# Single-precision zeros for the products that clear the counting banks of a four-layer graph network

## The reference, cut to what matters

```python
edge_index = jnp.stack([src, dst])
x = _layernorm(x + _L0_gnn_ref(x, edge_index, edge_attr_128, ...), axis=-1)
x = _layernorm(x + _L1_gnn_ref(x, edge_index, ...), axis=-1)      # two _gat_conv
x = _layernorm(x + _L2_gnn_ref(x, src, dst, ...), axis=-1)        # agg = segment_sum(h[src], dst)
x = _layernorm(x + _L3_gnn_ref(x, edge_attr_128, ..., src, dst), axis=-1)
```

## Time and profile before

| | us |
|---|---|
| median of three executions (lowest to highest) | 3548.91 (3539.84 to 3549.04) |
| the profiled execution | 3545.56 |
| its span | 3543.7 |
| TensorE busy (share of the span) | 2663.5 (75%) |
| VectorE busy | 2171.4 (61%) |
| ScalarE busy | 1652.8 (47%) |
| GpSimd busy | 1575.3 (44%) |

### The profile page before, as it was taken

How to read it: one execution, slowest core, us unless ns; L and a number is a source line. 1 busy time by engine, 2 the same in 40 slices (tenths; PEclk the granted TensorE clock), 3 DMA queues, 4 the chain that set the end, 5 groups by cost and what they waited for, 6 DMA issues and landing times.

```text
span 3543.7 us, 48598 instructions
## 1 busy us (share of the span) xinstructions
PE 2663.5 (75%) x11507; PEld 1959.5 (55%) x11507; DVE 2171.4 (61%) x5184; ACT 1652.8 (47%) x3627; POOL 1575.3 (44%) x1656
## 2 busy tenths in 40 slices
PE   6777778757777777567777764999998995677766
PEld 4665665434444444334444454777777884566654
DVE  5888886655555555645555567443455546666668
ACT  2887886434444444344444453442222344444443
POOL 4777770277765530177776530000000003777770
PEclk9999999855555555555555555999999997888886
DMA  6555550144443331244444321776677774555550
GB/s 205 155 160 156 161 159 27 38 107 103 99 98 95 89 75 37 58 105 101 99 100 96 89 67 56 246 270 206 225 265 260 270 281 158 154 159 154 159 153 25
DMA packets 391112, 489.16 MB, mean 138 GB/s; under 512 B 168377, under 2 KB 265710, under 8 KB 385888
## 3 DMA queue, kind: packets, MB, share of 16 engines
q1 hardware_dynamic: 324934, 288.34, 26.7%
q0 software_dynamic: 63088, 192.63, 19.9%
q10 hardware_dynamic: 2828, 5.18, 0.5%
HBM read 384.00 MB, written 101.90 MB: 137 GB/s over the span
## 4 chain that ended last, share of the span: by engine, by line
PE 43%; DVE 20%; POOL 12%; issue 10%; DMA 8%; ACT 3%; DVEq 2%; SPq 1%; ACTq 0%; POOLq 0%
PE ps L979 11%; POOL y_and_h L725 10%; DMA rows<-in_ea_swept 7%; PE ps L1060 7%; PE ps L995 6%; PE ps L857 6%; PE ps L991 4%; DVE y_and_h L1690 3%; DVE big L1662 3%; PE ps L943 2%; DVE ps L1682 2%; POOL big L711 2%; ACT w_sb L1419 2%; DVE ps L2169 1%; PE ps L793 1%
## 5 line engine op out<-in xcount | busy, mean ns | idle before, releaser
L711 POOL DMA_INDIRECT big<-table_gat,src_idx x832 | 809.3, 973 | 749.0 <-DMA table_gat<-y_and_h 343.2
L1662 DVE TENSOR_TENSOR big<-big,ps 128x257 f32 (+3 forms) x1664 | 592.6, 356 | 236.3 <-PE ps L979 17.4
L1419 ACT ACTIVATE w_sb<-ps 128x200 uint16 x784 | 262.1, 334 | 757.9 <-PE ps L995 756.7
L725 POOL DMA_INDIRECT y_and_h<-table_pool,src_block x391 | 374.8, 958 | 177.1 <-issue 118.9
L696 POOL DMA_INDIRECT big<-table_mlp,src_block x391 | 371.3, 950 | 158.1 <-issue 116.8
L1466 ACT ACTIVATE big<-big 128x3432 f32<-128x3432 uint16 (+1 forms) x72 | 210.1, 2919 | 476.7 <-PE ps L1060 476.7
L2023 DVE TENSOR_TENSOR big<-w_sb,extra 128x512 bf16<-128x512 bf16 (+1 forms) x392 | 179.1, 498 | 340.7 <-PE ps L995 340.5
L740 POOL DMA_DIRECT2D big<-adj x36 | 19.2, 533 | 802.1 <-ACT big L1466 703.8
L995 PE MATMUL ps<-big 128*128 128x200 bf16 x784 | 277.6, 354 | 77.8 <-ACT w_sb L1419 74.5
L857 PE MATMUL ps<-w_sb,ea_sb 128*128 128x256 f32 x832 | 210.2, 396 | 127.2 <-DVE y_and_h L1690 116.7
L1060 PE MATMUL ps<-big,y_and_h 128*128 128x264 f32 (+1 forms) x1200 | 289.4, 389 | 0.0
(11 more groups left out here) (344 smaller groups left out, 5162.8 us busy)
## 6 DMA issues: line engine op xcount, KB each, us to landing
big<-adj POOLq DMA_DIRECT2D x33, 1650.0 KB, 8.1
rows<-in_ea_swept SPq DMA_DIRECT2D x194, 256.0 KB, 3.4
adj<-w_sb SPq DMA_DIRECT2D x784, 50.0 KB
ea_sb<-in_ea_blocks SPq DMA_DIRECT2D x416, 64.0 KB
ea_sb<-rel_rows SPq DMA_DIRECT2D x208, 128.0 KB
prefix_blocks<-rows SPq DMA_DIRECT2D x97, 256.0 KB, 2.2
rows<-prefix_blocks SPq DMA_DIRECT2D x97, 256.0 KB, 3.5
below_blocks<-ea_sb SPq DMA_DIRECT2D x97, 256.0 KB, 2.7
```

The lines of the kernel that those rows point to most:

```text
L711: pool.indirect_dma_start(ring[:, step % GAT_RING, :], None, table[k], bass.IndirectOffsetOnAxis(src_idx[:, step:step + 1], 0))\
L725: pool.indirect_dma_start(pool_rows[q][:, i, :], None, table["pool"], bass.IndirectOffsetOnAxis(src_block[:, block:block + 1], 0)).then_in ...
L1419: act.activation(staging[:, (4 * quad + j) % STAGED, :], ps[:, 6:8, :][:, bass.ds(halves_of[j + 1], 1), 0:CW].rearrange("p o n -> p (o n)" ...
L1662: dve.tensor_tensor(to, to, bank_of(j), ALU.add).then_inc(accumulated, 1)
```

## The change

The clearing product of each counting step reads its two rows of zeros as single-precision words instead of as bfloat16 ones. Shapes (1 x 128 by 1 x 200), banks, waits and order stay, and so does the value, zero.

```diff
--- before.py
+++ after.py
@@ -309,7 +309,6 @@
         step_chunk, step_key = chain[:, 56:60], chain[:, 60:64]
         staging = w_sb[:, 0:STAGED * CW // 2].bitcast(U16).rearrange("p (s n) -> p s n", s=STAGED)
         count4 = w_sb[:, 1600:1600 + 2 * CW].bitcast(BF16).rearrange("p (n q) -> p n q", q=4)
-        zeros_b = zeros[:, :].bitcast(BF16)
         quads_at = GAT_RING_AT + GAT_RING * ROW["gat1"] + 256 * MARKS
         lo4 = [part_of_big(quads_at + b * 656, 256).bitcast(BF16).rearrange("p (n q) -> p n q", q=4) for b in range(2)]
         col4 = [part_of_big(quads_at + b * 656 + 256, 400).bitcast(BF16).rearrange("p (n q) -> p n q", q=4) for b in range(2)]
@@ -989,7 +988,7 @@
                     if j == 0:
                         pe.wait_ge(quad_ready, quad + 1)
                     pe.matmul(ps[:, 6:8, :][:, ::-1, :][:, bass.ds(halves_of[j], 1), 0:CW].rearrange("p o n -> p (o n)"),
-                              zeros_b[0:1, 0:P], zeros_b[0:1, 0:CW], start=True, stop=True, skip_group_check=True)
+                              zeros[0:1, 0:P], zeros[0:1, 0:CW], start=True, stop=True, skip_group_check=True)
                     if step:
                         pe.wait_ge(step_read, step)
                     pe.matmul(ps[:, 6:8, :][:, bass.ds(halves_of[j + 1], 1), 0:CW].rearrange("p o n -> p (o n)"),
```

## The result

The changed kernel takes 3884.68 us (median of 4 runs, 3881.96 to 3886.64) against 3544.38 us of the kernel before (4 runs, 3535.55 to 3549.04): a ratio of 1.096, 95% interval 1.094 to 1.099. It is slower by 340 us. The profiled executions, 3545.56 and 3881.96 us, differ by 336. The forecast was 3944 us with 3800 to 4020: the side and the range hold, and the sum is 59 us too large (395 against 336).

The account below looks back on a forecast made before the run. TensorE at 1.2 GHz was taken to bound both attention passes. 533 us of longer clearing products, less 86 (ScalarE), 37 (VectorE) and 15 (GpSimd) hidden, gave +395 us: forecast 3944 us, range 3800 to 4020.

Parts of the forecast that it names:

- What bounds the kernel: Both attention passes: TensorE at 1.2 GHz, 73% busy, its lines holding 63% and 56% of the chain of waits.
- Step 1: The bfloat16 clearing product in the passes today: 0.28 us from its weight load to the next product's.
- Step 2: Single-precision clearing product, priced from line 1235 in the last stage: 0.96 us, 0.68 added, times 784 is 533 us of TensorE.
- Step 3, ScalarE: Line 995's wait for ScalarE's read in 210 counting steps hides 0.41 us each of the longer product: 86 us.
- Step 3, VectorE and GpSimd: VectorE waits in `find_maxima` and `make_logits` groups hide 37 us; GpSimd's gathers at the start of pass 2 hide 15 us.
- The sum: Whole run: 533 us added on TensorE less 86, 37 and 15 us hidden gives +395 us.
- The check from the other side: Line 991 holds 138 of 220 us on the chain in both passes, 63%; that share of 533 is 335 us.
- A sign that was off: Line 991 was to hold some 30% of the chain in the two passes.
- (a): TensorE's granted clock rises in the passes and the run gets faster: -60 us, 3489 us; chance 0.07.
- (b): Clearing product's weight loads hide behind products: 0.50 us added instead of 0.68, +266, 3815 us; chance 0.14.
- (c): Nothing of the longer clearing product is covered, as ScalarE's or VectorE's waits move along: +533, 4082 us; chance 0.06.
- (d): A clearing product of one row is cheap in either type: 3549 us, same time; chance 0.03.

## Why the prediction was right, and where it was off

**What bounds the kernel**: right. TensorE's column of work in the two attention passes sets the time, and all +336 us lie there.

**Step 1 and Step 2**: right to the hundredth. 0.28 us before, 0.96 after, 784 times. The price of the nearest row, one row of single precision in the last stage, was the right one to take, and 0.78 from the products of 128 rows was not: these hide their weight loads and one-row products don't. (At 128 rows it is 0.67, so the 0.11 added there has no place either.) The same extrapolation would have failed at 72 columns (0.63 instead of 0.54); at 200 it holds.

**Step 3, ScalarE**: this is the term that was mis-sized, and the step of the prediction that failed. It reads "the longer product runs inside this wait and hides 0.41 us", for 210 steps. The wait was read rightly, 0.69 from clearing to counting, and so were the 86 us of it (+444 measured from clearing to counting, 447 in the sum). But what stands behind the wait was left out: in 186 groups, in 170 of which step 0 has such a wait, TensorE's sequencer, once ScalarE lets the counting product go, reads the tile numbers for `add_terms`, and the engine is idle until 1.21 us after the clearing product. The longer product covers that idle time too, 0.27 us more: 50 us in 186 groups, 54 by the account. The rows that show it were in the trace of the kernel before: from line 995 to line 943 it is 0.52 us (1088.96 - 1088.44), and from line 995 to the next clearing product 0.29 (1087.76 - 1087.47). I followed the wait to its end and not to the next instruction.

**Step 3, VectorE and GpSimd**: right in kind. The wait of line 979 in the `find_maxima` group goes from 1.04 to 0.23 us, and in the `make_logits` group from 1.93 to 1.25, so 0.81 and 0.68 hidden where 0.95 and 0.68 were taken. All waits ahead of the sums together give 42 us. Of these 11 are GpSimd's, the wait of 11.2 us of the earlier trace rows, which is gone; with the 4.5 us at line 952 that is the 15 us taken for GpSimd. VectorE's cover is then about 30 us where 37 were taken.

**The sum** with the measured terms is 533 - 89 - 54 - 42 - 5 = 343, and 336 was found. So the 59 us are the idle time at the register load (54), 3 more hidden by ScalarE, 5 between counting and clearing products and 7 from the rest (4.5 of them at line 952), less the 10 by which the cover ahead of the sums was taken too large.

**The check from the other side** (63% of 533 = 335 us, by the share of the chain) came out at the measured value. In a step 0 that waits, the chain of the kernel before goes through ScalarE's line 1419 and leaves the clearing product out whole, so the register load's cover was in the share. It deserved more weight than "agrees on the size", but a hit to 1 us is luck: by the same 63% the 512-column run would lose 0.26 x 784 x 0.63 = 128 us and the 72-column one 173, and they lost 123 and 161.

**A sign that was off**: line 991 was to hold some 30% of the chain in the passes, and its successor holds 40 and 43%.

**The rivals.** (a) fell: the clock is 0.50 at 90% busy, and at 91% with two one-row products. What the prediction gave as the reason against it, that one-row products seem to count for nothing, agrees with the runs with 1, 32, 72 and 128 rows: 0.50, 0.50, 0.55, 0.62. (Its price was also a little off: the 1.25 us that it takes from the earlier trace rows for a pair begin at the counting product and hold that product's 0.17 us.) In single precision with full height it happens as (a) described, a clock of 0.75 and a run faster than the kernel before, 3514.70 us. (b) fell for one row (0.96, not 0.78); the weight loads do hide with 72 rows and more. (c) and (d) fell by the same rows.

**What remains open**: why a load of 1 or 32 rows is not pulled ahead of a product of 128 rows, and one of 72 rows is; and what sets the clock. From 72 to 128 rows the weight load is hidden in both and the clock still rises, so there the height alone goes with it; between 32 and 72 rows the idle time ahead of the clearing product goes as well, and no run changes one without the other. No height between 32 and 72 rows was run.

## What to carry to other kernels

When an instruction is made longer inside a wait, follow the engine past the end of the wait to its next instruction: a register load or other work of the sequencer behind it is cover too, and the shares of the chain show it in one number. A product that does little work isn't cheap because it has one row; give it the height of its neighbours, so that its weight load hides behind them and the clock isn't held down: here that took 120 us off 3550, with the same instructions, by the estimate above some 84 of them through the weight load and 36 through the clock.

## What the runs showed of the hardware

- **Height and the clock.** Granted clock over 600 us of pass 1, the clearing product bfloat16 with 200 columns: 0.50 with 1 and 32 rows, 0.55 with 72, 0.62 with 128; single precision with 1, 72 and 128 rows 0.50, 0.60, 0.75. TensorE was busy 75, 75, 72 and 71%, and 89, 82 and 79%: the clock went up with the rows, while the busy share went down.
- **Height and the weight load.** Between products of 128 rows, a clearing product of 1 or 32 rows holds TensorE 0.28 us at 1.2 GHz, one of 72 or 128 rows 0.17. Ahead of the first two the weight loads also stand idle for 0.25 us.
- **Small products in single precision.** With one row the product takes two weight loads, 0.50 us together. 200 columns hold TensorE 0.96 us, 72 columns 0.63, and one in bfloat16 of 512 columns 0.54: the type costs more than the columns.
- **A register load on TensorE's sequencer** of four values takes 0.33 us. Behind a wait, `add_terms` came 0.52 us after the counting product with it and 0.13 us with the load moved ahead; 0.25 us where the clearing product ahead held 0.96 us, and 0.01 behind two of them.
